# Three attention slots instead of two beside each group of expert rows in a decoder layer

## The chip, the cores and the metric

One core of a Trainium2 chip runs the whole program in one launch. The metric is device time in microseconds: the median of three runs is given for the kernel before, and one more execution was taken with the profiler.

## What is computed

The reference is one layer of a decoder on x (16 sequences of 256 tokens, width 128), in float32:

```python
x = x + mixer(layernorm(x))                 # 256 channels, 16 states, scan over 256 tokens
x = x + attention(layernorm(x), context)    # 16 heads of 8, 64 keys, masked
x = x + experts(layernorm(x))               # 8 experts of 128-512-128, the best 2 of each token
```

The mixer is a selective state-space scan with a convolution of 4 taps and a gate. The experts' part takes for each of the 4096 tokens the two best of eight, runs relu(x W1 + b1) W2 + b2 for each, and adds the two with a softmax over their gate scores.

## The kernel before, in words

The batch is worked in eight rounds of two sequences (512 tokens). A round has 16 steps (`STEPS`); each step does one scan of 4 states by 256 tokens for 128 channels on VectorE (L1642), the decays for it on ScalarE (L1173), the products with C and a fold on GpSimd (L1433, L1438), and sums on TensorE. Every engine has its own instruction stream, written out by hand, and semaphores between them. Beside step k of round r stands a *slot* (r, k): TensorE, ScalarE, VectorE and GpSimd each do some pieces of the mixer's front of round r + 1, of the attention of round r - 1 and of the attention's end and the routing of round r - 2. So after the scans of round 7 there are still 32 slots without a scan: rounds "8" and "9", that is the attention of round 7, and the end and routing of rounds 6 and 7. They are numbered 0 to 31 (`LASTS`), and their content on each engine is in the functions `drain`.

Routing puts each token's row, by indirect DMAs from GpSimd (L1477, eight of 128 rows for a round), into a table `xsd` in DRAM, sorted by expert. The table has two parts: rounds 0 to 5, and rounds 6 and 7. A small computation on VectorE, `group_table` (L1903 to L1915), then finds the *groups*: 256 rows of one expert each, 31 in the first part and 15 in the second, 46 in all (`GROUPS`).

For a group j the SyncE queue loads its rows (`load_rows`, L548, 132 KB) and its expert's weights (`load_weights`, L556, 578 KB) into rings of seven. VectorE normalises the rows (`tile_norm`, L1923), TensorE turns them (`tile_in`, L1017), ScalarE copies them out of PSUM (L1396), TensorE makes the hidden layer (`tile_up`, 8 products of 256 columns, named Rp or Mb<-soft), ScalarE and VectorE each do half of the relu (L1403, L1937), TensorE makes the result (`tile_down`, 16 products, Rp<-BC,xh), VectorE adds the bias (`tile_out`, L1943), and GpSimd scatters the rows to `y2d` with two indirect DMAs (`tile_back`, L1557). `tile_out` of group j waits for the scatter of group j - 4. At the end the two results of each token are loaded and added (L1970).

The first part's groups are ready after the scans, while 32 slots remain. Slots 0 to 2 (`BEFORE = 3`) stand ahead of the groups; the others are dealt out over the groups by `slots_of`, which all four engines' loops call. On TensorE a group's turn is

```python
a, b = slots_of(j)
if j + 2 < GROUPS:
    tile_in(j + 2)
lasts(drain, a, b)
if j + 1 < GROUPS:
    tile_up(j + 1)
lasts(drain, b, b + 1)
tile_down(j)
```

ScalarE does relu(j), copy(j + 2) and then the slots a to b; VectorE relu(j), norm(j + 2), bias(j - 1) and then the slots; GpSimd the scatter of j - 1 and then the slots.

`group_of(r, k)` is the inverse: the group beside which slot (r, k) stands. It is used where the tiles and the routing share PSUM banks: L818 and L831 make the gate products (`scores_e`, slot 4 of rounds 8 and 9, that is slots 4 and 20) and the place counts (`places`, slots 11 and 27) wait until ScalarE has copied a certain tile, L1002 and L1003 make a later tile's transposes wait until VectorE has read the gates ("lg", slots 5 and 21) or the places ("pos", slots 12 and 28). L1986 puts the second group table one group after slot 28.

In the slots, TensorE's pieces are: scores_e and output products and the mixer's output (slot 4), keys, values and centring (6), variance (7), queries (8), scores (10 to 13), the turning of the maxima and the first transposed scores (14), three more of these (15 to 17), values (18), gates and output (20). ScalarE has the output copies (5), the spreads of the rows, copies of keys and values and a square (6), an inverse root and half of the key blocks (7), the other half (8), exponentials of the gates and the queries (9), and so on for round 7 in slots 17 to 25. VectorE has a selection in 10 and 26 and the maxima in 10 to 13. GpSimd's eight row scatters of a round are in slots 13 to 15 (2, 3, 3) and 29 to 31.

Of the kernel before, what the change touches and what calls it, by code (L numbers as in the profile page):

```python
# [20 lines left out]
ROUNDS = BATCH // NB  # L21
# [3 lines left out]
STEPS = CHUNKS * DT  # L25
# [37 lines left out]
BEFORE = 3  # L63
# [20 lines left out]
def decoder(nc, x, ctx_in, mask, ln_g, ln_b, W_in, W_x, W_dt, b_dt, W_out, conv_w, conv_b, A_log, D_param,  # L84
            alpha, w_q, b_q, w_k, b_k, w_v, b_v, w_o, b_o, W1, b1, W2, b2, Wg, bg,
            c_ident, c_center, c_mean, c_pick, c_pickmax, c_blk, c_iota, out):
    with ExitStack() as es:
# [324 lines left out]

        def slots_of(j):

            return BEFORE + 2 * j, BEFORE + 2 * j + 1

        def group_of(r, k):

            return ((r - ROUNDS) * STEPS + k - BEFORE) // 2

        def ahead(r):

# [200 lines left out]
        def _(pe):  # L623
# [186 lines left out]
            def scores_e(r):  # L810

                pe.wait_ge(Tv.sem, Tv.at("n", r))
                if r == 0:
                    pe.wait_ge(s_k, 3)
                if r + 3 < ROUNDS:
                    pe.wait_ge(Aa.sem, Aa.at("rs2", r + 3))
                if part_of(r):
                    pe.wait_ge(s_xg, group_of(r + 2, 4) + 3)  # L818
                for t in range(NTT):
                    to, tok = Gates[part_of(r)][:, t * (EXPERTS + 1):(t + 1) * (EXPERTS + 1)], slice(t * P, (t + 1) * P)  # L820
                    mm(to, oT[:, tok], wowg[:, :], stop=False)
                    m = mm(to, x1T[:, r % 2, tok], cwg[:, :], start=False)
                m.then_inc(Fp.sem, 1)

            def places(r):

                pe.wait_ge(Fv.sem, Fv.at("hot", r))
                if r + 3 < ROUNDS:
                    pe.wait_ge(Av.sem, Av.at("dt", r + 3))
                if part_of(r):  # L830
                    pe.wait_ge(s_xg, group_of(r + 2, 11) + 3)  # L831
                for c in range(2):
                    flat = hot[:, c, :, :].rearrange("p t e -> p (t e)")
                    for n in range(NTT + 1):
                        m = mm(Counts[part_of(r)], onesb[:, :] if n else tri[:, :],
                               flat[:, (NTT - n) * EXPERTS:(2 * NTT + 1 - n) * EXPERTS], start=n == 0 and c == 0, stop=n == NTT and c == 1)
                m.then_inc(Fp.sem, 1)
# [163 lines left out]
            for r in range(SPLIT, ROUNDS):  # L1001
                free[group_of(r + 2, 4) + 3] = Fv.at("lg", r)  # L1002
                free[group_of(r + 2, 11) + 3] = Fv.at("pos", r)  # L1003
# [47 lines left out]
            for j in range(GROUPS):  # L1051
# [8 lines that stand above are left out]
# [3 lines left out]
        def _(act):  # L1063
# [343 lines left out]
            for j in range(GROUPS):  # L1407
                a, b = slots_of(j)
                tile_relu(j)
                if j + 2 < GROUPS:  # L1410
                    tile_in(j + 2)
                lasts(drain, a, b + 1)
                if j == PARTS[1].group:
                    act.wait_ge(s_wt, 2)
                    A(wt[:, 1, :], wt[:, 1, :], ACT.Exp).then_inc(s_wt, 1)
# [3 lines left out]
        def _(pool):  # L1419
# [141 lines left out]
            for j in range(GROUPS):  # L1561
                a, b = slots_of(j)
                if j:
                    tile_back(j - 1)
                lasts(drain, a, b + 1)
# [472 lines left out]
```

## Time and profile before

| | before |
|---|---|
| median of 3 runs | 906.31 us (906.02 to 908.13) |
| the profiled execution's own time | 910.74 us |
| its span | 908.9 us |
| TensorE matmul busy | 728.1 us (80%) |
| VectorE busy | 716.1 us (79%) |
| GpSimd busy | 638.8 us (70%) |
| ScalarE busy | 530.6 us (58%) |
| mean granted TensorE clock | 0.925 |

Busy time is the union of an engine's instructions; the ends of matmuls are modelled, so that a matmul can stand in the trace as done before its result is reported to the engine that waits. The span runs from the first instruction to the last. DMA traffic is 148.91 MB, a mean of 164 GB/s.

### The profile page before, as it was taken

The numbers are of one execution on the slowest core, as the hardware profiler recorded it, in microseconds if no ns is written. First come the engines' busy times: TensorE is split into PE (matmuls) and PEld (weight loads), VectorE is DVE, ScalarE is ACT, GpSimd is POOL, SyncE is SP. The second block draws the span as 40 slices with busy tenths as digits, with TensorE's granted clock in tenths as the row PEclk, the third lists the DMA queues.
The fourth block names the chain that finished last, engine by engine and source line by source line (L and its number), as shares of the span: only waits on it lengthen the run. The fifth ranks groups of instructions, "written<-read, shape, count | busy, mean of one in ns | idle before, by whom it ended". The sixth has DMA issues, their size and how long they took to land. (4 is left out here: it accounts for less than half of the span.)

```text
span 908.9 us, 12684 instructions
## 1 busy us (share of the span) xinstructions
PE 728.1 (80%) x3977; PEld 494.9 (54%) x3977; DVE 716.1 (79%) x1060; ACT 530.6 (58%) x1272; POOL 638.8 (70%) x481
## 2 busy tenths in 40 slices
PE   4578669878888789788898878847798986999991
PEld 2354325445455455454545545524575785999981
DVE  3379999999999999999999999999336153555772
ACT  2667648767977966975976894680253331333320
POOL 1166989678889889898988988997323445545552
PEclk9679768999999999999979999987999998999997
DMA  3533775454546537446425633860633244785952
GB/s 97 184 108 102 213 241 183 151 179 140 174 130 203 173 114 224 132 157 206 152 96 161 201 111 113 283 188 25 211 108 113 96 153 141 252 268 167 372 160 71
DMA packets 83597, 148.91 MB, mean 164 GB/s; under 512 B 11137, under 2 KB 56079, under 8 KB 83530
## 3 DMA queue, kind: packets, MB, share of 16 engines
q1 hardware_dynamic: 78538, 139.55, 49.0%
q0 software_dynamic: 4992, 8.54, 2.7%
q8 instruction: 32, 0.52, 0.2%
q14 instruction: 35, 0.29, 0.1%
HBM read 115.34 MB, written 39.27 MB: 170 GB/s over the span
## 5 line engine op out<-in xcount | busy, mean ns | idle before, releaser
L1433 POOL TENSOR_TENSOR prod<-hst,BC 128x1024 f32<-128x1024 f32 x128 | 301.4, 2362 | 72.3 <-DVE hst L1642 63.2
L1642 DVE TENSOR_TENSOR_SCAN hst<-dA,Rp 128x1024 f32<-128x1024 f32 x128 | 292.2, 2283 | 6.4
L1173 ACT ACTIVATE dA<-dtm,Aneg 128x255 f32<-128x255 f32 x512 | 214.2, 495 | 67.2 <-DVE hst L1642 66.1
L1557 POOL DMA_INDIRECT y2d<-prod,back x92 | 91.6, 995 | 130.5 <-DVE prod L1943 112.7
L1438 POOL TENSOR_TENSOR prod<-prod 128x512 f32<-128x512 f32 x128 | 163.5, 1288 | 2.4
L1633 DVE TENSOR_TENSOR Rp<-BC,Rp 128x1024 f32<-128x1024 f32 x128 | 157.0, 1226 | 10.1 <-DMA BC<-bcd 2.9
L625 PE MATMUL Y<-prod,ident 128*128 128x256 f32 x512 | 144.1, 416 | 20.3 <-POOL prod L1438 15.5
L625 PEld LDWEIGHTS Y<-prod,ident 128*128 128x128 f32 x512 | 102.4, 208 | 56.7 <-POOL prod L1438 20.6
L625 PE MATMUL Mb<-hpad,winT 128*128 128x512 f32 (+1 forms) x176 | 82.5, 618 | 22.4 <-ACT xh L1122 14.2
L625 PE MATMUL Rp<-BC,xh 128*128 128x128 f32 x736 | 91.6, 278 | 7.4 <-DVE prod L1943 7.4
L625 PEld LDWEIGHTS Rp<-BC,xh 128*128 128x128 f32 x736 | 90.7, 195 | 12.0 <-issue 9.8
L1396 ACT ACTIVATE soft<-Y 128x256 f32<-128x256 f32 x44 | 16.9, 385 | 118.9 <-PE Y L1017 107.9
L1477 POOL DMA_INDIRECT xsd<-x2o,slots x64 | 63.2, 987 | 17.0 <-issue 16.6
L625 PE MATMUL T<-Kbd,qT 64*128 64x512 f32 x128 | 48.3, 686 | 27.9 <-DVE mx L1659 17.9
L625 PEld LDWEIGHTS Mb<-hpad,winT 128*128 128x128 f32 x176 | 36.1, 213 | 61.1 <-issue 27.0
L1943 DVE TENSOR_TENSOR prod<-Rp,BC 128x256 f32<-128x256 f32 x46 | 19.5, 425 | 47.2 <-PE Rp L625 30.8
L1221 ACT ACTIVATE E<-T 128x512 f32<-128x512 f32 x64 | 34.5, 589 | 34.0 <-PE T L625 24.8
L625 PE MATMUL T<-qT,Kbd 64*128 64x256 f32 x256 | 38.2, 419 | 16.2 <-ACT E L1221 14.8
L1659 DVE TENSOR_REDUCE mx<-T 128x8 f32<-128x512 f32 x64 | 40.7, 677 | 5.9 <-PE T L625 5.9
L625 PE MATMUL Mb<-soft,BC 128*128 128x256 f32 x184 | 45.3, 391 | 0.0
L625 PE MATMUL Rp<-soft,BC 128*128 128x256 f32 x184 | 43.6, 380 | 1.2 <-ACT soft L1396 1.2
L1937 DVE TENSOR_SCALAR xh<-Rp,BC 128x256 f32<-128x256 f32 x46 | 20.1, 478 | 27.9 <-PE Rp L625 25.0
(254 smaller groups left out, 1189.5 us busy)
## 6 DMA issues: line engine op xcount, KB each, us to landing
BC<-bcd SPq DMA_DIRECT2D x64, 1024.0 KB, 5.4
BC<-recs SPq DMA_DIRECT2D x46, 578.0 KB
xsd<-blank SPq DMA_DIRECT2D x18, 1056.0 KB, 12.4
dtm<-xsd SPq DMA_DIRECT2D x46, 132.0 KB
recs<-in_L_ffn_W SPq DMA_DIRECT2D x16, 256.0 KB
xin<-in_x SPq DMA_DIRECT2D x8, 256.0 KB, 5.0
x2d<-x2o SPq DMA_DIRECT2D x8, 256.0 KB, 5.6
E<-x2d SPq DMA_DIRECT2D x4, 512.0 KB
```

The source lines that it names most:

```text
L625: return pe.matmul(o, l, r_, start=start, stop=stop, **kw)
L1173: m = A(dA[:, k % RING, i, 1:SEQ], dtm[:, r % 2, d, b * SEQ + 1:(b + 1) * SEQ], ACT.Exp, scale=Aneg[:, d, c * NC + i:c * NC + i + 1])
L1221: m = A(E[:, b, hp:hp + 2, :], T[h][:, :].rearrange("p (i s) -> p i s", i=2), ACT.Exp)
L1433: TT(prod[:, k % RING, :, :], hst[:, k % RING, :, :], BC[:, (k // 2) % BCR, 1, :, :], ALU.mult).then_inc(s_pd, 1)
L1438: TT(prod[:, k % RING, 0:NC // 2, :], prod[:, k % RING, 0:NC // 2, :], prod[:, k % RING, NC // 2:NC, :], ALU.add).then_inc(s_fd, 1)
L1477: pool.indirect_dma_start(out=xsd[:, :], out_offset=bass.IndirectOffsetOnAxis(ap=slots[:, c, t:t + 1], axis=0), in_=x2o[:, t, :], in_offse ...
L1557: pool.indirect_dma_start(out=y2d[:, :], out_offset=bass.IndirectOffsetOnAxis(ap=at, axis=0), in_=yr[:, j % YR, i, :], in_offset=None, bou ...
L1633: v.tensor_tensor(U, BC[:, (k // 2) % BCR, 0, :, :], DTX[:, d, :].unsqueeze(1).to_broadcast([P, NC, SEQ]), ALU.mult).then_inc(s_u, 1)
L1642: v.tensor_tensor_scan(hst[:, k % RING].rearrange("p n s -> p (n s)"), dA[:, k % RING].rearrange("p n s -> p (n s)"), U.rearrange("p n s - ...
L1659: v.tensor_reduce(mx[:, i, h * 8:h * 8 + 8], T[h][:, :].rearrange("p (h k) -> p h k", k=KEYS), AX.X, ALU.max).then_inc(Tv.sem, 1)
L1937: v.tensor_scalar(hid[:, j % 2, c, :], Up[j % 2][1][:, i, :], b1r[:, j % RINGS, c:c + 1], 0.0, ALU.add, ALU.max).then_inc(s_rb, 1)
L1943: v.tensor_tensor(yr[:, j % YR, :, :], Down, b2r[:, j % RINGS, :].unsqueeze(1).to_broadcast([P, GT, D]), ALU.add).then_inc(s_ys, 1)
```

## The change

The two functions that tie slots and groups to each other use three slots for a group. Slots 3 to 31 then lie on groups 0 to 9 where they lay on 0 to 14. For group j, TensorE does the first two of its three slots between `tile_in(j + 2)` and `tile_up(j + 1)`, and the third between `tile_up(j + 1)` and `tile_down(j)`. The waits of L1002 and L1003 move from tiles 3, 7, 11 and 15 to tiles 3, 5, 8 and 11, those of L818 and L831 with them, and the second group table from group 13 to group 9.

```diff
@@ -412,11 +412,11 @@
 
         def slots_of(j):
 
-            return BEFORE + 2 * j, BEFORE + 2 * j + 1
+            return BEFORE + 3 * j, BEFORE + 3 * j + 2
 
         def group_of(r, k):
 
-            return ((r - ROUNDS) * STEPS + k - BEFORE) // 2
+            return ((r - ROUNDS) * STEPS + k - BEFORE) // 3
 
         def ahead(r):
 
```

## Rows read from the trace of the kernel before

**Rows 1.** Windows: busy time of each engine in a stretch, granted clock, DMA share.
```profile
669.00:686.00 17.00, 13.59 (x76) 10.66 (x78) 6.19 (x32) 15.59 (x54) 6.62 (x9) 1.00 0.51 157
...
773.00:836.00 63.00, 62.22 (x421) 58.60 (x422) 35.23 (x116) 20.25 (x52) 32.50 (x33) 0.97 0.77 244
```
**Rows 2.** Chain that ended last, in order of time: start, us, what.
```profile
803.41 3.51 PE Rp L625 x24
...
810.88 3.51 PE Rp L625 x24
```
**Rows 3.** Timeline of ScalarE: start, us, instruction, idle time before it.
```profile
671.28 0.41 ACT L1238 ACTIVATE sqs<-x2o 128x128 f32<-128x128 f32 x1
...
676.91 0.69 ACT L1087 ACTIVATE rstdt<-T,epsc 128x512 f32<-128x512 f32 x1 [0.21 <-PE T L625]
...
678.17 4.77 ACT L1210 ACTIVATE Kbd<-KT,blk 128x128 f32<-128x128 f32 x16
...
684.96 0.68 ACT L1093 ACTIVATE qT<-T,bq 128x512 f32<-128x512 f32 x1
```
**Rows 4.** Timeline of TensorE, 640 to 703 us.
```profile
646.52 0.64 PE L625 MATMUL T<-E,Vg 128*32 128x256 f32 x8 [1.17 <-ACT E L1221]
...
660.64 0.28 PE L625 MATMUL Y<-wowg,oT 128*128 128x9 f32 x2
...
666.78 1.95 PE L625 MATMUL Rp<-BC,xh 128*128 128x128 f32 x16
...
675.75 1.12 PE L625 MATMUL T<-sqt,mean 128*128 128x512 f32 x2 [0.58 <-ACT sqt L1082]
...
679.10 1.13 PE L625 MATMUL T<-sqt,attT 128*128 128x512 f32 x2 [0.50 <-DVE sqt L1654]
...
685.79 1.13 PE L625 MATMUL T<-Kbd,qT 64*128 64x512 f32 x4 [1.83 <-ACT qT L1093]
...
689.91 0.44 PE L1017 MATMUL Y<-ident,soft 128*128 128x128 f32 x2 [0.68 <-DVE soft L1923]
...
702.25 0.42 PE L768 MATMUL T<-identb,nm 128*96 128x128 bf16 x4 [0.41 <-DVE nm L1672]
```
**Rows 5.** Timeline of VectorE.
```profile
691.77 1.29 DVE L1659 TENSOR_REDUCE mx<-T 128x8 f32<-128x512 f32 x2 [1.24 <-PE T L625]
...
696.63 0.87 DVE L1937 TENSOR_SCALAR xh<-Mb,BC 128x256 f32<-128x256 f32 x2
697.42 0.59 DVE L1923 TENSOR_SCALAR soft<-dtm 128x128 f32<-128x128 f32 x2
```
**Rows 6.** Timeline of TensorE, 733 to 785 us.
```profile
735.18 0.41 PE L1017 MATMUL Y<-ident,soft 128*128 128x128 f32 x2 [0.78 <-DVE lg L1694]
...
747.73 0.44 PE L1017 MATMUL Y<-ident,soft 128*128 128x128 f32 x2 [1.03 <-DVE soft L1923]
748.73 0.18 PE L625 MATMUL Y<-hot,tri 128*128 128x40 bf16 x1 [0.56 <-ACT soft L1396]
...
748.98 3.58 PE L625 MATMUL Mb<-soft,BC 128*128 128x256 f32 x8
...
759.60 0.44 PE L1017 MATMUL Y<-ident,soft 128*128 128x128 f32 x2 [1.44 <-issue]
...
764.39 0.44 PE L1017 MATMUL Y<-ident,soft 128*128 128x128 f32 x2 [0.84 <-issue]
...
773.35 3.52 PE L625 MATMUL Rp<-BC,xh 128*128 128x128 f32 x16 [6.79 <-DVE prod L1943]
```
**Rows 7.** Timeline rows of three engines, and a window with the columns of rows 1.
```profile
707.96 1.08 ACT L1221 ACTIVATE E<-T 128x512 f32<-128x512 f32 x2 [4.66 <-remote]
...
758.24 0.97 POOL L1477 DMA_INDIRECT xsd<-x2o,slots  x1 [0.30 <-issue]
...
772.77 0.42 DVE L1943 TENSOR_TENSOR prod<-Rp,BC 128x256 f32<-128x256 f32 x1 [8.22 <-remote]
...
749.00:753.00 4.00, 4.00 (x19) 3.29 (x16) 1.12 (x6) 0.84 (x2) 2.20 (x3) 0.57 0.90 267
```

## The prediction

> **What bounds the kernel now.** I read the windows first, then the chain of waits, then the timeline of each engine in the stretch that the change touches. After the last scan TensorE (PE) has 46 expert groups to do, and the first fifteen, 0 to 14, carry the slots of the remaining attentions. Once the slots are done PE never rests: from 773 to 836 us it is busy for 62.22 of 63 us [rows 1], and the chain is PE alone: 3.51 us are a down product and the next up product, and the pattern of two groups returns after 810.88 - 803.41 = 7.47 us, 3.73 us a group [rows 2]. While the slots run, PE is not full: 13.59 of 17 us from 669 to 686, with ScalarE (ACT) at 15.59 [rows 1]. There ACT is the bound: the work of slots 5 to 9 stands in one queue, from the spreads at 671.28 over a root at 676.91 and 4.77 us of key blocks from 678.17, to the queries that leave at 684.96 [rows 3]. The groups' products are what PE does meanwhile. So each slot's length is set by a handover between engines, and each handover is as cheap as the tile work beside it.
>
> **The change part by part.** No instruction is added or dropped. The 29 slots from 3 to 31 lie on groups 0 to 9 instead of 0 to 14, and the third slot of a group follows the up product, so that two slots stand side by side in PE's queue where there was one, with no product between them. Total work is the same; the time changes by PE's waits alone. I lay the queues with the durations of the rows.
>
> *Slot 4, group 0.* The gate products start at 660.64, behind an up product; now they stand right behind the transposes of tile 2 and wait for ACT's copy of that tile, as the place counts do at 748.73, for 0.56 us [rows 6]; I take 0.6, from 659.0 to 659.6. They and the two output products take 666.78 - 660.64 = 6.14 us [rows 4] and end at 665.7; up and down products follow, to 669.3.
>
> *Slots 6 to 8, group 1.* Slot 5's two copies on ACT are done early, so spreads begins at 670.0 (behind the copy of tile 3) instead of 671.28. From its start to the variance product is 675.75 - 671.28 = 4.47 us [rows 3, 4], so this product comes at 674.5. PE, however, has only 1.5 us of key, value and centring products after 669.7: it waits 3.35 us (0.58 before). Then variance to 675.5, up product to 677.2, 0.65 us of wait for the normalised input (0.50 before), query product and down product to 680.6, next transposes to 681.0.
>
> *Slot 10, group 2.* ACT has root, key blocks, a relu and a copy, exponentials and queries from 675.6 on; with the rows' durations, PE may start the scores at 684.6 (685.79 before). It waits 3.6 us (1.83 before). The two groups' worth of products that stood there are no longer in front. Sum of these waits: 0.6 + 3.35 + 0.65 + 3.6 = 8.2 us, against 0.58 + 0.50 + 1.83 and one wait of 0.77 for the logits, 3.7 us, the same kind as the first of [rows 6], which falls away in group 1. Cost: +4.5 us.
>
> *Slots 10 to 14, groups 2 and 3.* VectorE (DVE) sets a new wait: the transposes of tile 5 now need the places of round 6, slot 12, the first of the same group. Before them in DVE's queue are the maxima of slot 11 (1.29 us), a relu (0.87), the norm (0.59) [rows 5], and three short ones, the tile's bias and the places among them: 693.1, against a PE that is free at 691.4: 1.75 us. Scores 3 directly behind scores 2 wait 0.65 us for maxima 2, the turning of the maxima 0.6 and the first transposed scores 0.7. Together 3.7 us, against 2.45 us (three waits of 0.68 and one of 0.41 [rows 4]): +1.25 us.
>
> *Slots 15 to 20, groups 4 and 5.* Transposed scores directly behind their predecessor wait for its exponentials: 1.17 us, as in [rows 4] at 646.52, where no tile work stood between. Once in group 4; in group 5 the gate product of slot 20 has only an up product between it and the values and waits some 0.4 us. +1.6 us.
>
> *Slots 21 to 31.* These take groups 6 to 9 instead of 9 to 14. Their waits belong to the code and not to the filling: the logits (0.78), the norm behind the selection (1.03), a copy (0.56), the second group table (1.44) and the tile behind it (0.84), 4.65 us in all [rows 6]. I get 4.6 us again. At 748.98 the up product took 3.58 us instead of 1.89: PE ran at half clock there [rows 6, 7], 1.85 us; I keep one such loss. Change: 0.
>
> *The other queues.* SyncE's loads are tied to groups; its two stores of residuals (round 6 and 7) find their data earlier. Row loads of the second part need the table by group 24, which is far. GpSimd has the same indirect transfers at 1.27 us each (0.97 and a gap of 0.30 [rows 7]); in group 9 six row scatters now stand in a row, 7.6 us, before the next tile's scatter. The bias of a tile waits only for the scatter of four groups earlier, 14.9 us, so this costs nothing; without that cover it would cost up to 7.6 us. The end after 889 us hangs on group 45 as before.
>
> Sum: 4.5 + 1.25 + 1.6 + 0 = 7.35 us on the profiled execution, which took 910.74 us (span 908.9); the runs' median is 906.31. The waits don't depend on that offset, so I add them to the median: **913.6 us**. Bounds: if every new wait is half as long, +3.7; if two of them are paid twice over, at half clock, +11.
>
> [...]
>
> **The rivals.**
> *Half clock behind the new waits.* Place: products after 674.5 and 684.6. For it: PE is sparsely used from 669 to 686. Against: the first one is partly hidden by ACT's queue. 2 times 1.85 us more: 917.3 us at most, 915.5 with one.
> *The late results of PE.* At 764.39 PE turned the next tile and an up product followed, yet its next down product began only at 773.35, after 6.79 us of wait put down to DVE [rows 6]; DVE itself waited 8.22 us for a product that stands in the trace as long done, while GpSimd issued scatters, those of rows from 758.24 on [rows 7]. Beside round 6's scatters ACT waited 4.66 us for transposed scores [rows 7], of which I put half, some 2.4 us, down to the same stall. If PE's results are held up by a long row of scatters, the new order, which splits the last eight as two and six and puts them elsewhere, may remove up to 8.2 + 2.4 = 10.6 us: 913.6 - 10.6 = 903.0 us. This is the case that ends faster; it decides from 10.0 us saved on, and from 4.6 us saved it gives no change. Against: all sixteen scatters are still issued just as densely. [...]
> *The slots' end counts, not their filling.* With the same PE work, the hand schedule's waits may overlap with ones already there, so that only the 3.5 us of the ACT queue remain or less: +2, 908.3 us.
> *The change has no effect on the order.* Excluded: the same function gives the slots to all four queues.
>
> **How the numbers follow.** A measurement can tell about 0.3% here, 2.7 us, from no change. Forecast, +5 to +9: 0.42. Longer, by half clock or a longer stall: 0.15. Smaller but slower, +2.7 to +5: 0.16. No change, from overlapping waits or half of the late results gone: 0.16. Faster: 0.11. So faster 0.11, same 0.16, slower 0.73. The range leaves the outermost tenths out: 905.5 to 917.5 us.
>
> **What would show it.** Right: PE's wait before the variance product grows to over 3 us and before the first scores to over 3 us; a wait of 1 to 2 us before tile 5's transposes; slot 31 in group 9; group 10 onward at 3.73 us. Wrong: ACT no longer full in 670 to 684 us, or no stall like that of 764 to 773 us beside the last scatters, or the clock at one half in 675 to 690 us.

## The result and the profile after

| | before | after |
|---|---|---|
| median | 907.22 us (4 runs, 906.02 to 911.55) | 920.11 us (4 runs, 918.76 to 921.0) |
| ratio to before, 95% | | 1.0134 [1.011, 1.0159] |
| profiled execution, its span | 910.74, 908.9 us | 918.76, 917.0 us |

Slower by 12.9 us between the medians; 7.35 was forecast, and 920.11 lies outside the range. The two profiled executions differ by 8.0 us only, because that of before was 3.5 us above its median and that of after 1.35 us below its own. I read the trace in the order of the forecast. First the timeline of TensorE (PE) of after, for the places of [rows 4] and [rows 6] (start, length, instruction, idle time before it and who ended it):

```profile
655.78 0.44 PE L1017 MATMUL Y<-ident,soft 128*128 128x128 f32 x2 [1.29 <-DVE soft L1923]
656.78 0.36 PE L625 MATMUL Y<-wowg,oT 128*128 128x9 f32 x2 [0.56 <-DVE oT L1678]
...
674.95 2.08 PE L625 MATMUL T<-sqt,mean 128*128 128x512 f32 x2 [3.24 <-ACT sqt L1082]
...
685.92 2.08 PE L625 MATMUL T<-Kbd,qT 64*128 64x512 f32 x4 [3.55 <-ACT qT L1093]
...
697.06 0.41 PE L1017 MATMUL Y<-ident,soft 128*128 128x128 f32 x2 [1.21 <-DVE sq L1729]
699.63 1.72 PE L625 MATMUL T<-Kbd,qT 64*128 64x512 f32 x4 [0.57 <-DVE mx L1659]
...
712.58 1.13 PE L625 MATMUL T<-qT,Kbd 64*128 64x256 f32 x8 [1.17 <-ACT E L1221]
...
727.42 0.39 PE L625 MATMUL Y<-wowg,oT 128*128 128x9 f32 x2 [0.54 <-DVE oT L1678]
```

The two long waits and two of the short ones stand where they were forecast: 3.24 for 3.35 us, 3.55 for 3.6, 0.56 for 0.6, 1.17 for 1.17; the others are set against the forecast further down. But look at the second number. The variance product and the first scores took 2.08 us where they took 1.12 and 1.13 before [rows 4]. The windows of after (engines as in rows 1, then granted clock, DMA share, GB/s) say why:

```profile
655.00:658.00 3.00, 1.66 (x12) 1.45 (x12) 1.63 (x6) 0.78 (x3) 0.00 (x0) 0.94 0.61 227
658.00:665.00 7.00, 7.00 (x28) 5.84 (x27) 0.26 (x2) 0.60 (x1) 0.00 (x0) 0.54 0.00 0
665.00:675.00 10.00, 6.76 (x39) 5.01 (x37) 2.30 (x8) 5.98 (x20) 2.65 (x5) 0.98 0.34 96
675.00:678.00 3.00, 3.00 (x5) 1.79 (x6) 0.00 (x0) 0.91 (x2) 0.00 (x0) 0.50 0.15 54
678.00:685.00 7.00, 4.38 (x26) 3.19 (x25) 2.86 (x8) 7.00 (x27) 1.30 (x2) 0.99 0.15 44
685.00:692.00 7.00, 6.08 (x14) 3.37 (x14) 2.72 (x17) 1.62 (x5) 1.03 (x3) 0.52 0.23 81
692.00:729.00 37.00, 31.75 (x269) 22.25 (x269) 13.89 (x42) 9.38 (x20) 13.91 (x15) 1.00 0.27 82
729.00:733.00 4.00, 4.00 (x23) 4.00 (x23) 0.00 (x0) 0.00 (x0) 0.00 (x0) 0.57 0.00 0
```

Four stretches at half clock, in slots 4, 7, 10 and 20, with PE busy for 7.00 + 3.00 + 6.08 + 4.00 = 20.08 us in them. Before, the clock was whole in all of this time:

```profile
640.00:749.00 109.00, 93.70 (x721) 73.07 (x721) 42.55 (x155) 41.90 (x124) 36.73 (x45) 1.00 0.44 141
```

**Where the time went.** I cut both traces at two points: the start of tile 2's transposes (658.63 before, 655.78 after; the change acts only from there) and PE's end of slot 20's output products. These rows of the two timelines, before first, are the second point:

```profile
732.23 0.39 PE L625 MATMUL T<-ident,x1T 128*128 128x128 f32 x2
```
```profile
732.29 0.59 PE L625 MATMUL T<-ident,x1T 128*128 128x128 f32 x2
```

From point to point it is 73.99 us before and 77.10 after. Before has finished eight groups by then, after five, so a group's 3.73 us is taken off for each: 44.1 us of slots before, 58.5 after, +14.3. The waits over 0.4 us inside are 8.14 us before and 12.60 after, +4.5. The clock is the rest, 9.8 us, and half of the 20.08 busy us is 10.0 (with the granted clock of each of the four rows instead of one half, 9.4): the account closes. Behind slot 20, up to the bias of group 45, after is 3.2 us shorter, mostly in one stall. VectorE's timeline of after shows it at 5.43 us, for 8.22 in [rows 7]:

```profile
766.84 0.42 DVE L1943 TENSOR_TENSOR prod<-Rp,BC 128x256 f32<-128x256 f32 x1 [5.43 <-remote]
```

VectorE's bias waits for two things, PE's product and the scatter of four groups earlier, so a late scatter would be an explanation too. ScalarE's copy of the next tile waits for products of PE only (the semaphores of the transposes and of an up product), and it is released within 0.05 us of the bias, before first:

```profile
772.82 0.38 ACT L1396 ACTIVATE soft<-Y 128x256 f32<-128x256 f32 x1 [11.04 <-remote]
```
```profile
766.88 0.38 ACT L1396 ACTIVATE soft<-Y 128x256 f32<-128x256 f32 x1 [8.19 <-remote]
```

So what came late was PE's results, and not that scatter. In all, the change costs 14.3 - 3.2 = 11.1 us in this pair of traces; after had come to the first cut point 2.85 us earlier, ahead of anything that the change acts on, and that leaves the 8 us between the two executions.

At this point two explanations stood. The clock: without its falls the change would cost only its waits. The density itself: the waits and the crowding cost it all, and the clock merely falls inside time that is idle anyway. A third question was open beside them, the rival of the late results: what the stall of 8.22 us in [rows 7] is.

### The profile page after: what moved, and what is told of

It reads as the page before. It is cut to its first block and busy times, and to the rows that moved or that the text cites. A ratio compares the mean times of both kernels' runs of the same rounds, so it can differ in the third digit from the quotient of the medians.

```text
span 917.0 us, 12684 instructions
## 1 busy us (share of the span) xinstructions
PE 732.3 (80%) x3977; PEld 499.7 (54%) x3977; DVE 716.8 (78%) x1060; ACT 531.2 (58%) x1272; POOL 637.3 (70%) x481
## 5 line engine op out<-in xcount | busy, mean ns | idle before, releaser
L625 PE MATMUL Y<-prod,ident 128*128 128x256 f32 x512 | 141.2, 409 | 23.9 <-POOL prod L1438 19.0
L625 PEld LDWEIGHTS Y<-prod,ident 128*128 128x128 f32 x512 | 100.5, 204 | 59.4 <-POOL prod L1438 23.9
L625 PE MATMUL T<-Kbd,qT 64*128 64x512 f32 x128 | 50.4, 686 | 31.1 <-DVE mx L1659 19.5
L1937 DVE TENSOR_SCALAR xh<-Mb,BC 128x256 f32<-128x256 f32 x46 | 20.1, 479 | 40.1 <-PE Mb L625 31.8
L625 PE MATMUL Rp<-soft,BC 128*128 128x256 f32 x184 | 44.3, 384 | 1.2 <-ACT soft L1396 1.2
## 6 DMA issues: line engine op xcount, KB each, us to landing
xsd<-blank SPq DMA_DIRECT2D x18, 1056.0 KB, 12.4
```

Of the source, the lines that this page charges most:

```text
L625: return pe.matmul(o, l, r_, start=start, stop=stop, **kw)
L1937: v.tensor_scalar(hid[:, j % 2, c, :], Up[j % 2][1][:, i, :], b1r[:, j % RINGS, c:c + 1], 0.0, ALU.add, ALU.max).then_inc(s_rb, 1)
```

## The experiments

The expectations are quoted as written before the runs. Kernels that ran in one session share the runs of before: late3b to fill4b, split to sparse_spread, and again with split_fill. The column "early" is the 44.1 or 58.5 us above (between the two cut points, less 3.73 us a finished group), "late" runs from there to the start of VectorE's bias of group 45, plus 3.73 us for each group already finished at the second point, so that both columns compare the same work; both are of the one profiled execution, in us.

| kernel | ratio, 95% | early | late, whole |
|---|---|---|---|
| before | | 44.1 | 188.2 |
| after | 1.0134 [1.011, 1.0159] | 58.5 | 185.0 |
| late3b | 0.998 [0.9955, 1.0005] | 42.9 | 187.5 |
| early3b | 1.0163 [1.0142, 1.0184] | 58.4 | 187.4 |
| fill2b | 1.0092 [1.0065, 1.0118] | 54.4 | 185.1 |
| fill4b | 1.0104 [1.0083, 1.0126] | 52.6 | 188.1 |
| split | 1.0045 [1.0026, 1.0064] | 51.2 | 185.8 |
| spread | 0.9978 [0.9955, 1.0] | 44.1 | 184.6 |
| late3_spread | 0.9992 [0.9974, 1.0009] | 44.2 | 186.0 |
| sparse_spread | 0.9967 [0.9945, 0.999] | 44.3 | 183.8 |
| again (last session) | 1.0154 [1.0118, 1.0189] | 54.8 | 177.6 |
| split_fill (last session) | 1.0085 [1.0052, 1.0118] | 48.4 | 176.5 |

How far one trace can be trusted: the kernels that have the order of before up to slot 20 (before, late3b, spread, late3_spread) lie between 42.9 and 44.2 us early, those with the order of after (after, early3b, again) at 58.5, 58.4 and 54.8.

### Which slots cost it: late3b and early3b

late3b keeps two slots a group up to slot 20 and gives three from slot 21 on; early3b does the reverse. Both replace the formula by a list:

```diff
+PLAN = [[3 + 2 * j, 4 + 2 * j] for j in range(9)] + [[21, 22, 23], [24, 25, 26], [27, 28, 29], [30, 31]]
-            return BEFORE + 2 * j, BEFORE + 2 * j + 1
+            return (PLAN[j][0], PLAN[j][-1]) if j < len(PLAN) else (LASTS, LASTS)
-            return ((r - ROUNDS) * STEPS + k - BEFORE) // 2
+            n = (r - ROUNDS) * STEPS + k
+            return next(j for j, at in enumerate(PLAN) if n in at)
```

The list of early3b is `[[3 + 3 * j, 4 + 3 * j, 5 + 3 * j] for j in range(6)]` and then pairs from 21 to 31.

> Two slots beside each group up to slot 20, as before the change, and three only for slots 21 to 31 (groups 9 to 12). If the cost is paid where the attention is dense (waits and half clock of slots 3 to 20), this kernel lies within 2 us of the kernel before. If the later end of cover for the routing slots counts, it carries a share of the 12 to 13 us: 3 us or more.

> Three slots beside each group up to slot 20, as in the change, and two from slot 21 on (groups 6 to 11). The complement of the kernel with three slots for the late ones alone: by the first theory it costs all that the change costs, 11 to 14 us over the kernel before; by the rival at most 9 us.

late3b took 906.26 us against 908.26 of before, no measurable difference; early3b 922.94, +14.7 us. So the whole price sits in slots 3 to 20, and three slots a group are free from 21 on, as the "Change: 0" said of the waits there. early3b has the same early part as after, 58.4 to 58.5 us, and its trace has the four half-clock stretches again: granted 0.51 in 659 to 666 us, 0.52 in 676 to 679, 0.50 in 688 to 692 and 0.59 in 730 to 734.

### Does the clock cost it: fill2b and fill4b

fill2b is the changed kernel with spare products put into the two long waits, into a bank of PSUM that is overwritten next; they compute nothing that is used.

```diff
+            def warm(n):
+                for _ in range(n):
+                    mm(M[0], onesb[0:96, :], selmax[:, 0:4, :].rearrange("p g k -> p (g k)"))
...
+                        pe.wait_ge(s_ra, 4)
+                        pe.wait_ge(s_rb, 4)
+                        warm(10)
...
+                    if k == 10:
+                        warm(12)
```

The first three added lines of the second part stand ahead of the variance product of slot 7. fill4b has, besides, `warm(5)` ahead of the gate products of slots 4 and 20, behind waits for what these products will need.

> The changed kernel with 10 spare bf16 products of 512 columns (results not used) in TensorE's queue ahead of the variance product of slot 7, where it waits 3.24 us, and 12 ahead of slot 10, where it waits 3.55 us. They fit into these waits at full clock (some 0.22 us each). If the half clock of 675 to 678 and 685 to 692 us comes from the idle time before it, both stretches show a granted clock of 1.00 and the kernel is 3 to 4 us faster than the change. If only the waits themselves count, the time stays or grows by up to 1 us, and the half clock with it.

> As the kernel with products in slots 7 and 10, and 5 more such products ahead of the gate products of slot 4 and of slot 20, where the clock fell in 658 to 664 and 729 to 733 us. They take some 1.1 us each time, of which a wait of 0.55 us covers half. If dense work before the thin gate products (9 columns) keeps the clock, 3 to 5 us more are won than with slots 7 and 10 alone, less the 1.1 us that the products cost: 5 to 8 us faster than the change in all. If the thin products themselves lower the clock, it is as slow as with slots 7 and 10 alone, or 1 us slower.

TensorE's timeline of fill2b:

```profile
677.74 1.12 PE L625 MATMUL T<-sqt,mean 128*128 128x512 f32 x2 [1.08 <-ACT sqt L1091]
...
687.76 1.13 PE L625 MATMUL T<-Kbd,qT 64*128 64x512 f32 x4 [0.96 <-ACT qT L1102]
```

The variance product comes no earlier, 19.2 us behind the first cut point in both (the wait is for ScalarE), but the two products take 1.12 and 1.13 us again, not 2.08, and the windows of fill2b have the clock whole from slot 6 to slot 19, with the loss of slot 4 left, and that of slot 20:

```profile
660.00:667.00 7.00, 7.00 (x32) 6.43 (x32) 0.26 (x2) 0.60 (x1) 0.00 (x0) 0.53 0.01 4
667.00:728.00 61.00, 53.22 (x373) 35.69 (x372) 21.69 (x75) 24.91 (x72) 18.94 (x24) 1.00 0.27 83
728.00:732.00 4.00, 4.00 (x23) 4.00 (x23) 0.00 (x0) 0.00 (x0) 0.00 (x0) 0.58 0.00 0
```

Early part 54.4 for 58.5 us, 4.1 less: half of the 3.00 + 6.08 busy us of slots 7 and 10 is 4.5. So of the two outcomes written down for fill2b the first came for the clock: granted 1.00 in 677 to 681 and in 687 to 692 us, for 0.50 and 0.52 behind the same two waits of after. Work was added and time was won, which crowding alone can't give. The totals agree: 917.47 us against 922.94 of early3b in the same session, of which the stall behind slot 20 has a share, and 1.0092 for the 1.0134 of after, about 3.8 us less, though these two intervals just overlap. fill4b takes another 1.8 us off the early part, since slot 4 keeps its clock for the gate products (granted 1.00 in 655.8 to 658.2 us) and loses it for the output products only (the half-clock window of 4 us there, 0.57 in 658.5 to 662.5 us, replaces one of 7) and slot 20 loses none (1.00 in 720 to 727 us). Its total was no better than that of fill2b, 917.61 to 917.47 us, where 5 to 8 us less than the change had been expected (the ratios differ by 0.3%, 2.7 us): in its trace the late part is 3 us longer. So the second half of the effect rests on the clock in the windows of one trace; its 1.8 us alone are within what the same order differs by from trace to trace.

### Both causes at once: split

The changed kernel with the up product in two halves, one between each pair of slots, so that no two slots stand side by side in PE's queue.

```diff
-            def tile_up(j):
+            def tile_up(j, halves=(0, 1)):
-                for half, (filled, emptied) in enumerate(((s_ua, s_ra), (s_ub, s_rb))):
+                for half in halves:
+                    filled, emptied = ((s_ua, s_ra), (s_ub, s_rb))[half]
...
-                lasts(drain, a, b)
+                lasts(drain, a, a + 1)
-                    tile_up(j + 1)
+                    tile_up(j + 1, (0,))
+                lasts(drain, a + 1, b)
+                if j + 1 < GROUPS:
+                    tile_up(j + 1, (1,))
```

> The changed kernel with TensorE's up product cut in two: the first half stands between the first and the second slot of a group, the other half ahead of the third, so that no two slots stand side by side. The work is the same. Each half is 0.87 us at full clock. If the cost comes from slots side by side, the waits of 0.56 (slot 4), 3.24 (7), 3.55 (10), 0.57 (13) and 1.17 us (16) fall by up to 0.87 us each, some 3.7 us together, and with dense products there one or more of the half clocks go: 4 to 8 us faster than the change. If only the number of groups beside the slots counts, it stays within 2 us of the change.

913.27 us against 908.14: of the 12.9 us some 5 are left. The same start of slot 4 as in the first fence above, now with half an up product in it (timeline of TensorE in split):

```profile
657.43 0.44 PE L1017 MATMUL Y<-ident,soft 128*128 128x128 f32 x2 [1.30 <-DVE soft L1927]
657.70 1.03 PE L625 MATMUL Mb<-soft,BC 128*128 128x256 f32 x4
658.57 0.28 PE L625 MATMUL Y<-wowg,oT 128*128 128x9 f32 x2
...
660.80 0.39 PE L625 MATMUL T<-attT,oT 128*128 128x128 f32 x2
...
672.51 1.76 PE L625 MATMUL T<-sqt,mean 128*128 128x512 f32 x2 [2.37 <-ACT sqt L1086]
...
683.17 2.08 PE L625 MATMUL T<-Kbd,qT 64*128 64x512 f32 x4 [2.68 <-ACT qT L1097]
...
723.39 0.39 PE L625 MATMUL Y<-wowg,oT 128*128 128x9 f32 x2 [0.55 <-DVE oT L1682]
...
726.40 0.39 PE L625 MATMUL T<-ident,x1T 128*128 128x128 f32 x2
```

The wait of 0.56 us is gone and the clock holds (granted 1.00 in 655 to 665 us): pairs of output products take 0.39 us, where after has 0.63. The half up product stands where that wait was, so this run doesn't tell which of the two the clock answers to. And slot 20 warns against a simple rule: its wait of 0.55 us and its thin products of 9 columns stand in split as in after, and here the clock held (1.00 in 720 to 727 us). Behind 2.37 and 2.68 us of wait it fell all the same (0.50 in 673 to 676 us, 0.57 in 683 to 687), and once more from 700 to 704 us (0.57), where after has it whole (1.00 from 692 to 729).

### The late results: spread, late3_spread, sparse_spread

spread is the kernel before with the second eight row scatters of GpSimd one a group, over groups 13 to 20, instead of in slots 29 to 31.

```diff
-                    if k >= STEPS - 3:
+                    if k >= STEPS - 3 and r == ROUNDS:
...
+                if 0 <= j - group_of(ROUNDS + 1, 13) < 2 * NTT:
+                    scatter(ROUNDS - 1, j - group_of(ROUNDS + 1, 13))
```

late3_spread is late3b with the same edit. sparse_spread has it too, and gives slots 7, 8 and 9, where ScalarE is the bound [rows 3], a group each:

```diff
+PLAN = [[3, 4], [5, 6], [7], [8], [9]] + [[10 + 2 * j, 11 + 2 * j] for j in range(11)]
```

> The kernel before with the last round's eight row scatters one beside each of groups 13 to 20, in place of five and three beside 13 and 14. If TensorE's late results at 764 to 773 us come from the run of scatters, the stall of 8.2 us goes with it: 4 to 8 us faster than before, and no granted half clock behind it. If they come from something else there, the stall stays and the time is within 2 us of before.

> Three slots a group for slots 21 to 31 alone, and the eight scatters one beside each of groups 11 to 18. If the two edits add up: as the kernel before with spread scatters, or up to 2 us faster. If density in the late slots does cost and was covered by the stall, it is 1 to 3 us slower than that kernel.

> The other way round: slots 7, 8 and 9, in which ScalarE is full, get a group each, all others two a group (31 in group 15), with the scatters one beside each of groups 14 to 21. If TensorE's waits there (0.58, 0.50 and 1.83 us before) are only for want of tile products, they go and the kernel is 1 to 3 us faster than the kernel before with spread scatters. If ScalarE's queue grows by the relus and copies of the added groups as fast as the cover does, there is no gain, within 1 us.

VectorE's timeline of spread:

```profile
765.26 0.42 DVE L1945 TENSOR_TENSOR prod<-Rp,BC 128x256 f32<-128x256 f32 x1 [1.93 <-remote]
...
775.05 0.42 DVE L1945 TENSOR_TENSOR prod<-Rp,BC 128x256 f32<-128x256 f32 x1 [3.24 <-remote]
...
784.86 0.42 DVE L1945 TENSOR_TENSOR prod<-Rp,BC 128x256 f32<-128x256 f32 x1 [3.25 <-remote]
```

One stall of 8.22 us has become several of 2 to 3 us, further apart, and the window from 640 to 836 us of this trace has a granted clock of 1.00. The late part is 3.6 us shorter and the median 905.33 for 908.14 us; its interval reaches just to 1, and the 4 to 8 us that were expected did not come. ScalarE's copies are released with the bias here too (775.09 for 775.05 us). late3_spread, with 907.23 us, shows no difference from before; its interval overlaps that of spread, so whether the two edits add up is not settled. sparse_spread has the lowest ratio of this study, 905.08 for 908.14 us, 0.9967 [0.9945, 0.999], and can't be told from spread. Its timeline in the place of [rows 4] has the variance product behind dense tile work, without a wait worth a row:

```profile
672.14 1.89 PE L627 MATMUL Mb<-soft,BC 128*128 128x256 f32 x8
673.87 1.02 PE L627 MATMUL T<-sqt,mean 128*128 128x512 f32 x2
```

Yet its early part is no shorter than that of before (44.3 for 44.1): what slots 7 to 9 won came back as a wait of 3.08 us at 715.00 and a half-clock stretch behind it (granted 0.50 in 716 to 719 us). So its gain is that of the scatters, as far as one trace tells, and its slot list is worth nothing that these runs can show.

### The changed kernel again, and split with filling

split_fill adds `warm(7)` and `warm(9)` to split, in slots 7 and 10, as in fill2b. The changed kernel ran beside it once more.

> The changed kernel with the up product in halves and, beside that, 7 and 9 spare products in the waits of slots 7 and 10 (2.37 and 2.68 us there). With the halves alone the clock was at one half in 673 to 676, 683 to 687 and 700 to 704 us. If idle time lowers it, the first two go, and the kernel is 2 to 4 us faster than with the halves alone, within 3 us of the kernel before: what then remains over it is TensorE's longer waits. If the clock falls there for another reason, the time is that of the halves alone or up to 1 us longer.

> The changed kernel once more, beside the other runs on the same chip: 1.01 to 1.016 times the kernel before. If the half clocks of slots 4, 7, 10 and 20 follow from the order of the work, they stand in this profile too, within 3 us of the same work; if they are chance, some are missing and others new.

In the session of these two runs the kernel before took 893.29 us (7 runs), 14 to 15 us less than in the other sessions, so their totals can be set only against each other and against this before: again 905.73, split_fill 901.04. They ran on a chip of the same number, 2, as split and spread, so the chip alone doesn't explain the step. The trace of again repeats the waits line by line:

```profile
654.72 0.36 PE L625 MATMUL Y<-wowg,oT 128*128 128x9 f32 x2 [0.56 <-DVE oT L1678]
...
657.25 0.39 PE L625 MATMUL T<-ident,x1T 128*128 128x128 f32 x2
657.47 0.54 PE L625 MATMUL T<-attT,oT 128*128 128x128 f32 x2
657.81 0.64 PE L625 MATMUL T<-ident,x1T 128*128 128x128 f32 x2
...
671.27 2.07 PE L625 MATMUL T<-sqt,mean 128*128 128x512 f32 x2 [3.23 <-ACT sqt L1082]
...
682.24 2.08 PE L625 MATMUL T<-Kbd,qT 64*128 64x512 f32 x4 [3.54 <-ACT qT L1093]
```

The four stretches at half clock are there too, that of slot 4 shorter: the clock falls 2.75 us behind the first thin product, where after, early3b and fill2b have it 0.7 us behind; granted are 0.50 in 658 to 661 us, 0.54 in 671 to 674, 0.50 in 682 to 688 and 0.60 in 725 to 729. This last one, in slot 20, is behind a wait of only 0.18 us. In split_fill the clock is whole (1.00) from 640 to 699 us and PE's three waits are short (0.87, 1.36 and 0.74 us); the early part is 6.4 us shorter than that of again. The total gained 4.7 us and stays 0.85%, 7.75 us, above before, more than the early part of 48.4 against the 44.1 of the trace of before explains (again: 12.4 us above, of which 10.7 are early). It had been expected within 3 us of before and 2 to 4 us faster than split; against before of its own session it is no better than split (1.0085 for 1.0045), so the totals don't bear out the second. What the rest is I can't say, since the kernel before has no trace from that session.

What again settles is the stall. From 729 to 836 us PE was busy for 102.96 of 107 us:

```profile
729.00:836.00 107.00, 102.96 (x716) 96.23 (x715) 62.73 (x225) 36.88 (x101) 61.17 (x68) 1.00 0.70 224
```

There was no wait for a product long done, with the same scatters in the same slots, and the late part came out at 177.6 for 185.0 us; split_fill has none either, while every trace of the other sessions has, with a longest wait of VectorE of 3.25 (spread) to 8.80 us (late3b). So the stall beside the scatters isn't a property of this order of work alone.

## Why the prediction was half right

**What held.** The mechanism and the sign: PE's waits grow where two slots stand side by side, in slots 4, 7 and 10, the two long ones and the first put there to 0.1 us by laying the queues by hand. The end from slot 21 on: three slots a group cost nothing there, as late3b shows. "Group 10 onward at 3.73 us" holds as well. The rival that the change would have no effect, or that only the ends count, fell.

**The waits, by their terms.** Slots 4 to 10: +4.5 forecast, 7.35 - 3.68 = +3.7 measured; the 0.65 us before the query product did not come, since the variance and up products in front of it ran at half clock. Slots 10 to 14: +1.25 forecast, 2.88 - 2.45 = +0.4; the transposes of tile 5 waited 1.21 us, not 1.75. Slots 15 to 20: +1.6 forecast, +0.4 measured. Here a step was wrong: it counted the new waits (1.17, 0.54, and 0.66 not foreseen) against nothing, but the trace of before has two of that kind, which I had left out:

```profile
709.10 1.14 PE L625 MATMUL T<-qT,Kbd 64*128 64x256 f32 x8 [1.55 <-ACT E L1221]
...
717.61 1.13 PE L625 MATMUL T<-qT,Kbd 64*128 64x256 f32 x8 [0.46 <-ACT E L1221]
```

Together +4.5 for +7.35 us: this term was too large, and the waits of before to which it was held were not all there.

**The step that failed** is "I keep one such loss": a half-clock price of 0 for the new waits, with a rival that charged at most 2 times 1.85 us at 0.15. Measured were four stretches and 9.8 us. Three things were wrong in it. The weight: the row of before that speaks against a fall, 1.83 us of wait with the clock at 1.00 [rows 1, 4], has two groups of dense products around it, and the change takes just those away; [rows 6, 7] have 0.57 behind shorter waits, of 1.03 and 0.56 us. The places: I looked only at the two long waits and not at slots 4 and 20, where a wait of some 0.5 us now stands right ahead of thin products of 9 columns; they hold 11.0 of the 20.08 busy us. That packing brings these two falls the runs show (none in before, late3b and spread, both in each of after, early3b, fill2b and again); whether the wait or the thin products do it they leave open. The price: 1.85 us was to be the loss of one up product, which is 3.58 - 1.89 = 1.69 us in [rows 6], and a stretch here lasted 3 to 7 us, with PE busy in nearly all of it. The two errors have opposite signs: with both right the forecast would have been 906.31 + 4.5 + 9.8 = 920.6 us. That this lies so near to the 920.11 measured is partly luck, since the stall gave back 3.2 us that nobody forecast and the runs of before have a median of 907.22 with the fourth.

The forecast's own signs said so: the clock at one half between 675 and 690 us was named as one of being wrong, and it came (0.50 and 0.52). ScalarE, whose queue was to stay full, was busy for 13.14 of the 17 us of [rows 1], for 15.59.

Behind the two long waits the granted clock was 0.50 and 0.52 in after (3.24 and 3.55 us), 0.52 and 0.50 in early3b (3.24 and 3.54 us), 0.54 and 0.50 in again (3.23 and 3.54 us). With the rival's two losses of 1.85 us taken in, the forecast would have been 3.7 us higher, which is the right direction and still short: the stretches of slots 7 and 10 alone cost 4.5 us, by half their busy time, and those of slots 4 and 20 come on top.

**The late results of PE.** The stall stayed (5.43 for 8.22 us), spreading the scatters split it up, and in the last session it was absent with the scatters unchanged. That it is the scatters that hold results up is not shown, and not refuted: they set where it falls, but something else decides whether it comes. The products themselves are hardly slower there (in spread the down products beside the stalls take 2.02 us, for 1.95 elsewhere), which doesn't explain the wait. The cause stays open.

## What to carry to other kernels

Where an engine's dense work is what hides handovers between others, price packing the handovers closer in two parts: the waits, by laying the queues by hand, and half of the busy time behind each wait, if the clock is seen to fall (here to 0.50 to 0.60 for 3 to 7 us at a time). Ask of each handover what dense product still stands directly around it, also of the short ones; here the clock held in slot 4 (1.00 in split, 0.54 in after) with half an up product in place of a short wait, and spare products in the two long waits paid for themselves (4.1 us off the early part in fill2b). Expect the short ones to be hard to foretell: slot 20 lost the clock in four traces of the packed order (granted 0.57 to 0.60) and held it in split and split_fill (1.00). And list the waits of before in the whole stretch, not only those that the argument needs.

## What the runs showed of the hardware

- Behind waits of 1.29 and 0.56 us with only two transposes between them, and then products of 9 columns, the clock fell to one half: 0.7 us behind the first of these products in after, early3b and fill2b (granted 0.54, 0.51 and 0.53 over 7 us), 2.75 us behind it in again (0.50 in 658 to 661 us). With a half up product of 1.03 us in place of the second wait, in split, it held (1.00 in 655 to 665 us).
- The same thin products behind one wait in slot 20 lost the clock in after (wait of 0.54 us, granted 0.57) and again (0.18 us, 0.60) and kept it in split (0.55 us, 1.00) and split_fill (0.18 us, 1.00).
- In split waits of 2.37 and 2.68 us were followed by a granted clock of 0.61 and 0.57 over 4 us.
- Ten and twelve spare bf16 products of 512 columns in waits of over 3 us kept the clock in fill2b (1.00 in 667 to 728 us, for 0.50 in 675 to 678 and 0.52 in 685 to 692 in after) and took 4.1 us off the early part.
- VectorE waited 8.22 us in the trace of before and 5.43 us in that of after for products that stand there as long done, with ScalarE released within 0.05 us, and not at all in that of again, which is the same program as after; its late part was 7.4 us shorter there.
